# Cross-attention on one core: values two heads behind the scores, more heads multiplied whole

## The reference, cut to what matters

```python
scores = jnp.einsum('bhqd,bhkd->bhqk', q, k) * scale
probs = jax.nn.softmax(scores, axis=-1)
out = jnp.einsum('bhqk,bhkd->bhqd', probs, v)
out = out.transpose(0, 2, 1, 3).reshape(b, sq, DIM)
return out @ Wo
```

## Time and profile before

| what | value |
|---|---|
| median of 3 runs | 2446.28 us |
| profiled execution: its own time | 2448.94 us |
| profiled execution: span | 2447.2 us |
| granted TensorE clock, mean of the span | 0.995 |
| TensorE matmul busy | 2396.4 us (98%) |
| VectorE, ScalarE, GpSimd busy | 1272.9, 1049.7, 1382.5 us |
| `attend_pass` in the span | about 1840 to 2223 us |

### The profile page before, as it was taken

The page is one execution under the profiler, slowest core; times in us unless marked ns, Lnnn a source line. Parts: engine busy times, 40 slices in busy tenths (PEclk is TensorE's granted clock), DMA queues, the critical chain, the costliest instruction groups (busy, mean ns, idle before and its releaser), DMA issues. The chain is left out here.

```text
span 2447.2 us, 33141 instructions
## 1 busy us (share of the span) xinstructions
PE 2396.4 (98%) x12798; PEld 2098.0 (86%) x12798; DVE 1272.9 (52%) x1791; ACT 1049.7 (43%) x1542; POOL 1382.5 (56%) x627
## 2 busy tenths in 40 slices
PE   9999999999999999999999999999999999999998
PEld 9999999988899989999889999899986777666776
DVE  5862303862016940039720069434547899895666
ACT  2112234533337342346333363323327888882111
POOL 5434244865446855448655468444437999981221
PEclk9999999999999999999999999999999999999999
DMA  7656632334323333323333323378986776767763
GB/s 227 190 173 183 195 118 91 108 118 131 119 95 104 127 109 113 113 95 112 117 124 118 104 97 110 93 217 267 293 239 173 196 207 191 200 169 192 179 169 99
DMA packets 256158, 371.74 MB, mean 152 GB/s; under 512 B 127200, under 2 KB 179424, under 8 KB 255744
## 3 DMA queue, kind: packets, MB, share of 16 engines
q1 hardware_dynamic: 256000, 369.61, 50.4%
HBM read 290.15 MB, written 78.70 MB: 151 GB/s over the span
## 5 line engine op out<-in xcount | busy, mean ns | idle before, releaser
L1028 POOL TENSOR_TENSOR gp_w_lo<-cy_raw,gp_w_hi 128x1024 fp32r<-128x1024 f32 (+2 forms) x299 | 721.6, 2415 | 609.0 <-ACT gp_w_hi L903 608.5
L187 PE MATMUL gp_acc<-gp_x_hi,gp_w_hi 128*128 128x448 f32 x1504 | 558.0, 371 | 2.6 <-ACT gp_row L954 2.5
L189 PE MATMUL gp_acc<-gp_x_hi,gp_w_lo 128*128 128x448 f32 x1504 | 549.7, 365 | 0.0
L188 PE MATMUL gp_acc<-gp_x_lo,gp_w_hi 128*128 128x448 f32 x1504 | 549.6, 365 | 0.0
L903 ACT CAST gp_w_hi<-cy_raw 128x1024 fp32r<-128x1024 f32 (+2 forms) x300 | 307.1, 1026 | 313.1 <-PE gp_acc L189 307.5
L1511 POOL TENSOR_TENSOR ap_e_lo<-ap_e,ap_e_hi 125x1344 fp32r<-125x1344 f32 x104 | 317.2, 3092 | 9.9 <-DVE ap_e_hi L1593 6.9
L187 PEld LDWEIGHTS gp_acc<-gp_x_hi,gp_w_hi 128*128 128x128 f32 x1504 | 282.7, 188 | 25.8 <-ACT gp_row L954 4.0
L189 PEld LDWEIGHTS gp_acc<-gp_x_hi,gp_w_lo 128*128 128x128 f32 x1504 | 282.5, 188 | 22.1
L188 PEld LDWEIGHTS gp_acc<-gp_x_lo,gp_w_hi 128*128 128x128 f32 x1504 | 282.9, 188 | 20.9
L514 DVE TENSOR_REDUCE gp_sel_unit<-gp_keys 112x4 f32<-112x2048 f32 x4 | 9.1, 2286 | 548.4 <-ACT gp_keys L915 548.4
L187 PE MATMUL gp_acc<-gp_h_hi,gp_w_hi 128*128 128x448 f32 (+1 forms) x704 | 267.9, 381 | 8.4 <-DVE gp_h_lo L1091 5.6
(11 more groups left out here) (222 smaller groups left out, 4307.2 us busy)
## 6 DMA issues: line engine op xcount, KB each, us to landing
cy_raw<-in_w_gu SPq DMA_DIRECT2D x172, 512.0 KB, 3.2
cy_raw<-in_w_d SPq DMA_DIRECT2D x80, 512.0 KB, 3.5
cp_c_raw<-in_ctx_t SPq DMA_DIRECT2D x30, 750.0 KB, 6.7
cy_raw<-in_w_q SPq DMA_DIRECT2D x32, 512.0 KB, 4.5
q_scratch<-gp_q_out SPq DMA_DIRECT2D x64, 224.0 KB, 6.1
cy_qs<-q_scratch SPq DMA_DIRECT2D x64, 224.0 KB, 3.4
k_scratch<-cp_k_out SPq DMA_DIRECT2D x32, 376.0 KB
cy_ks<-k_scratch SPq DMA_DIRECT2D x64, 188.0 KB, 4.0
```

The lines of the kernel that those rows point to most:

```text
L187: nc.tensor.matmul(out, wh, xh, start=first, stop=False)
L188: nc.tensor.matmul(out, wh, xl, start=False, stop=False)
L189: return nc.tensor.matmul(out, wl, xh, start=False, stop=last)
L1028: last = nc.gpsimd.tensor_tensor(o, i, hi.bitcast(F32), ALU.subtract)
```

## The change

- `LAG` goes from 3 to 2: in the slot of head g TensorE multiplies the values of head g - 2. `take` and `put_o` follow from the same constant.
- `FULL` becomes `WHOLE`, the number of a head's blocks that are multiplied whole, the last ones of the head: 3 for head 3 as before, and 1 for head 7. In the last batch heads 1, 3, 5 and 7 are whole.
- `parts(g)` is the number of split blocks. `e_hi` and `e_lo` are made for those blocks only. `values` goes through a list: first the whole blocks, then `e_hi`, then `e_lo`. A head with one whole block has five matmuls, one in the first step and two in each of the others.
- `invert` goes from x = 22 to x = 20, behind `max_lo` and so ahead of `split_hi` of head 6; `put_recip` stays at h = 7.

```diff
-    LAG = 3
+    LAG = 2
-    RECIP_AT = 22
+    RECIP_AT, RECIP_PUT_AT = 20, 7
-    FULL, FULL_LAST = (3,), (3, 7)
+    WHOLE, WHOLE_LAST = (0, 0, 0, 3, 0, 0, 0, 1), (0, 3, 0, 3, 0, 3, 0, 3)
...
+    def parts(g):
+        return KT - (WHOLE if g // KV < B - 1 else WHOLE_LAST)[g % KV]
     def split(g):
-        return g % KV not in (FULL if g // KV < B - 1 else FULL_LAST)
+        return parts(g) > 0
...
-                nc.scalar.copy(e_hi[g % NHI][:], e[g % NE][:]).then_inc(hi_act, 1)
+                t = slice(0, parts(g))
+                nc.scalar.copy(e_hi[g % NHI][:, t], e[g % NE][:, t]).then_inc(hi_act, 1)
...
+                    if x == TURN_AT + 2 and n + 1 < B:
+                        max_lo(n + 1)
                     if x == RECIP_AT and n % GB == 0 and n > 0:
                         invert(n // GB - 1)
-                    if x == TURN_AT + 2 and n + 1 < B:
-                        max_lo(n + 1)
...
             def values(g, i):
+                s, vb, po = parts(g), vs[n % 2], p_o[g % 2][0:VW, 0:T]
+                todo = [(0, t) for t in range(s, KT)] + [(1, t) for t in range(s)] + [(2, t) for t in range(s)]
+                bounds = {KT: (0, 2, 4, 6), KT - 1: (0, 1, 3, 5), 0: (0, 1, 2, 3)}[s]
...
+                for z in range(bounds[i], bounds[i + 1]):
+                    kind, t = todo[z]
+                    if z == 0 and kind == 0:
+                        pe.wait_ge(exped, KT * (g + 1))
+                    if kind == 1 and t == 0:
+                        await_hi(pe, g)
+                    if kind == 2 and t == 0:
+                        await_lo(pe, g)
```

More of the change, by code:

```diff
@@ L1485, in _ @@
                         put_o((KV * n + h - LAG) // 2 - 1)
-                    if h == RECIP_AT // KT and n % GB == 0 and n > 0:
+                    if h == RECIP_PUT_AT and n % GB == 0 and n > 0:
                         put_recip(n // GB - 1)
@@ L1510, in _ @@
                         pool.wait_ge(pv, g - NLO + 1)
-                    nc.gpsimd.tensor_tensor(e_lo[g % NLO][:], e[g % NE][:], e_hi[g % NHI][:].bitcast(F32),
+                    t = slice(0, parts(g))
+                    nc.gpsimd.tensor_tensor(e_lo[g % NLO][:, t], e[g % NE][:, t], e_hi[g % NHI][:, t].bitcast(F32),
                                             ALU.subtract).then_inc(lo_pool, 1)
@@ L1526, in exp @@
                 if x % KT == 0 and g >= NE:
-                    if not split(g - NE):
+                    if parts(g - NE) < KT:
                         act.wait_ge(pv, g - NE + 1)
@@ L1592, in split_hi @@
                     dve.wait_ge(hi_dve, upto(hi_by_dve, g) - 1)
-                nc.vector.tensor_scalar(e_hi[g % NHI][:], e[g % NE][:], 1.0, None, ALU.mult, ALU.add,
+                t = slice(0, parts(g))
+                nc.vector.tensor_scalar(e_hi[g % NHI][:, t], e[g % NE][:, t], 1.0, None, ALU.mult, ALU.add,
                                         accum_out=e_sum[:]).then_inc(hi_dve, 1)
@@ L1610, in split_lo @@
                 dve.wait_ge(pv, g - NLO + 1)
-                nc.vector.tensor_tensor(e_lo[g % NLO][:], e[g % NE][:], e_hi[g % NHI][:].bitcast(F32),
+                t = slice(0, parts(g))
+                nc.vector.tensor_tensor(e_lo[g % NLO][:, t], e[g % NE][:, t], e_hi[g % NHI][:, t].bitcast(F32),
                                         ALU.subtract).then_inc(lo_dve, 1)
@@ L1675, in values @@
                         pe.wait_ge(o_taken, g - 1)
[L1676 to L1681, removed]
-                        await_lo(pe, g)
-                    part = e_hi[g % NHI] if z < KT else e_lo[g % NLO]
-                    last = nc.tensor.matmul(p_o[g % 2][0:VW, 0:T], vs[n % 2][:, z % KT, h, :], part[:, z % KT, :],
-                                            start=(z == 0), stop=(z == 2 * KT - 1))
+                for z in range(bounds[i], bounds[i + 1]):
[5 more added lines that the diff above has]
+                    if kind == 2 and t == 0:
+                        await_lo(pe, g)
+                    flags = {"start": z == 0, "stop": z == len(todo) - 1}
+                    if kind == 0:
+                        last = nc.tensor.matmul(po, vb[:, t, h, :].bitcast(F32), e[g % NE][:, t, :], **flags)
+                    else:
+                        part = e_hi[g % NHI] if kind == 1 else e_lo[g % NLO]
+                        last = nc.tensor.matmul(po, vb[:, t, h, :], part[:, t, :], **flags)
                 if i == KT - 1:
```

## The result

The changed kernel takes 2513.8 us in the median of four runs (2510.8 to 2516.2), against 2446.1 for the kernel before: a ratio of 1.0274, 95% interval 1.0261 to 1.0286. It is slower by 67.7 us where 52.9 were forecast. 2513.8 lies inside the stated range of 2474 to 2524, and 0.8 us above 2513, the upper bound that the prediction gave the closed path by itself. The profiled execution took 2510.8 us, with a span of 2509.0; it is the fastest of the four.

The account below looks back on a forecast made before the run. GpSimd was taken to bound the attention pass, TensorE a close second; with LAG = 2 latency would decide. 55.2 + 1.3 - 5.4 + 1.8 = +52.9 us on 2446.3 gives 2499 us, range 2474 to 2524.

Parts of the forecast that it names:

- the closed path: Attention pass: scores, exponential, e_hi, e_lo, values, scores two heads on; 27.0 us a batch, bounds 2487 and 2513.
- four links: Closed path, heads 6 to 0, 0 to 2, 2 to 4, 4 to 6: 6.33, 7.4, 6.5 and 6.5 us.
- The other signs: Steady batches: GpSimd about 81% busy, TensorE waiting some 4.5 us a batch for e_lo, no pairs waiting for maxima.
- the clock of 1.00: TensorE's granted clock: forecast to stay at 1.00 in the changed kernel.
- SP's stores move by nothing: SP's queue: put_recip stays at h = 7, put_o moves to other slots with room; no cost.
- Reciprocals: Three instructions of 0.84 us ahead of e_hi of head 6, 0.2 of it hidden: 3 x 0.6 = +1.8 us.
- +55.2: Steady batches: 14 batches going from 23.06 to 27.0 us each, +55.2 us.
- First and last batch: Start of the pass, later first turn: +1.3 us; end, one head less in the tail and VectorE freed: -5.4 us.
- Throughput decides: Rival, attention pass: e_lo comes in time, subtraction 2.1 us, TensorE's 22.4 us is the batch; 2432 us, 6%.
- The subtraction gets faster: Rival, GpSimd's subtraction: 2.6 us as engines thin out, batch of 25.2 us; 2474 us, 7%.
- The clock falls: Rival, TensorE: standing lowers the granted clock once a batch, up to 25 us more; 2523 us, 8%.

Follow-up runs that it names:

- e3_v_early: The changed kernel with the load of the values issued at h = 4 in place of h = 7: 2499.3 us, ratio 1.0209.
- e1_lag3: The changed kernel with LAG back at 3, all other parts of the change kept: 2435.9 us, ratio 0.9949.
- e2_only_lag2: The kernel before with LAG = 2 and nothing else changed: 2519.6 us, ratio 1.0291.
- e4_short_lo: e3_v_early with GpSimd subtracting only each split head's first block, which TensorE's other e_lo matmuls read again: 2437.4 us, ratio 0.9959.
- e7_lag3_last_as_before: e1_lag3 with the last batch's whole heads as before, 3 and 7 only: 2435.4 us, ratio 0.9969.
- e8_lag2_recip22: e3_v_early with the reciprocals at x = 22 again in place of x = 20: 2500.9 us, ratio 1.0234.

## Why the prediction was right

**The closed path.** Right in its parts and in its sum: four links predicted at 26.75 and 27.0 with the queue, measured 26.95, and 26.93 to 27.01 in 13 batches of e3_v_early. Only the last 0.2 is partly luck: it was put down to `e_lo` of head 5 holding up head 6, and that is some 0.05 us (e3_v_early); three of the links are 0.07 to 0.1 us longer than counted, one 0.06 shorter. e1_lag3 and e2_only_lag2 pin the loss on LAG, and e4_short_lo pins it on the length of the links. The other signs came too: in e3_v_early GpSimd is busy 80.5% (81 forecast), TensorE stands 3.9 us a batch (4.5 forecast), for six `e_lo` a batch, and no pair waits 0.1 us or more for maxima. Only the clock of 1.00 did not come in the changed kernel, where it was 0.97.

**What was missed.** "SP's stores move by nothing: ... on a queue with room" looked at what SP stores, and not at what it loads. Of a lag that shrinks, the load of the values is a part: TensorE needs them one head sooner. And the other slots of `put_o` were not without effect: its two stores now stand ahead of the load and delay its issue by 1.47 us. No run changed that order alone, so how much of the loss is theirs is open. The late load was worth 9.9 us in the profiled execution, with the clock that fell behind the longest stands. This sum is not a fixed price: e2_only_lag2 issues the load just as late, and its stands for it are 0.94 us or less.

**Reciprocals.** The step that three instructions of 0.84 us "now stand ahead of `e_hi` of head 6, which lies on the closed path", +1.8, was wrong: they cost nothing at x = 20. At x = 22 they had cost 2.3 us, which are in the mean of 23.06 and so in the +55.2 already; the term ought to have been nothing. The batch with the reciprocal had rows of its own before, 0.7 to 1.0 us longer than its neighbours, and I had taken one mean, 23.06, over all.

**First and last batch.** +1.3 was forecast for the first; measured +0.1, but the moment at which the pass starts differs more than that from one trace to the next (first turns at 1854 to 1867 us), so this term was not to be tested. The last was forecast at -5.4 and measured -5.1. I named the shorter tail first and a VectorE freed of two subtractions second; it is the other way round. With LAG = 3 and the whole heads the end is 29.1 us (e1_lag3), no longer than with LAG = 2, and without them 33.8 (e7_lag3_last_as_before). VectorE's longest subtraction there is 3.48 us, as before, and 1.56 in the changed kernel. It goes with GpSimd's first subtraction for `finish_pass`; the kernel before, then the changed one:

```profile
2211.49 2.36 POOL L1514 TENSOR_TENSOR cy_o_lo<-cy_num,cy_o_hi 128x1024 fp32r<-128x1024 f32 x1 [18.25 <-ACT cy_o_hi L1568]
2211.77 3.49 DVE L1611 TENSOR_TENSOR ap_e_lo<-ap_e,ap_e_hi 125x1344 fp32r<-125x1344 f32 x1
```

```profile
2278.53 1.56 DVE L1620 TENSOR_TENSOR ap_e_lo<-ap_e,ap_e_hi 125x1344 fp32r<-125x1344 f32 x1
2279.66 2.64 POOL L1520 TENSOR_TENSOR cy_o_lo<-cy_num,cy_o_hi 128x1024 fp32r<-128x1024 f32 x1 [18.97 <-ACT cy_o_hi L1575]
```

The one that starts second is the longer for it, VectorE's before and GpSimd's after.

**Sum.** Forecast 55.2 + 1.3 - 5.4 + 1.8 = 52.9; measured in the traces 67.7 + 0.1 - 5.1 = 62.7, the spans differing by 61.8. The 9.8 us between the two sums look like the 9.9 of the load, but only because the rest cancels: +2.8 for the first interval and +0.3 for the last batch against -1.8, -1.2 and -0.3 for the reciprocals, the first batch and the eight plain intervals. By the medians the forecast was short by 14.6 us (2499.2 against 2513.8): 8.9 by the spans, and the other 5.7 because the profiled execution before lay 2.9 us above its median and the one after 3.0 below. The time lies in the range because the range had been widened for the falling clock; for the load that made the excess nothing had been set aside, and in that the range was lucky.

**Rivals.** *Throughput decides* had the right conditional: with a short subtraction (1.15 us) LAG = 2 gives 2437 us, near its 2432; the 2.1 us that it named as the point was not run. *The subtraction gets faster* is out, at 3.07 us with GpSimd 78% busy. *The clock falls* was right as to a fact and for the most part wrong as to its cause: it fell six times, five of them behind stands of 1.7 to 3.1 us for a load and once behind 1.64 us for `e_lo`, and not once a batch by frequent short ones, of which e3_v_early has as many at a clock of 1.00. The rule quoted there from the Trainium skill (TensorE: Matmul & The Clock Gate, "A second HAM failure mode: psum-queue depth-cycling"), that frequent short idle times make the clock swing, is not borne out by these stands, of some 4 us in each batch and up to 1.3 us at a time. But one of the 14 stands of 1.26 to 1.28 us in e8_lag2_recip22 was followed by a fall, so stands of this size are not safe either.

## What to carry to other kernels

When a pipeline's lag is cut, don't compare busy times; add up the latency from a step back to itself, hand-overs included, and count the heads it spans. Where the sum exceeds the bound engine's time for as many heads, the lag is too short, whatever the busy shares say. Then list everything whose due time the lag sets, the loads too: what was issued one stage ahead may now be late. And look at what the lag moves on the queue that issues the loads, since a store that changes its slot can come to stand ahead of one.

## What the runs showed of the hardware

- TensorE stood 54 of 379 us, once for 1.64 us and else for 1.3 or less, and kept the full clock (e3_v_early: 1.00). After each of five stands of 1.7 to 3.1 us in the changed kernel the granted clock was near 0.5 for about 3 us, after each of three of 2.03 or 2.04 us in e2_only_lag2 for about 6 us; that kernel's other stands for `e_lo`, up to 1.57 us and one of 1.64, had no such fall. The stand of 1.64 us at the start of the pass was followed by a fall in one of the four traces with LAG = 2 that have it.
- GpSimd's subtraction of 125 x 1344 elements takes 3.07 to 3.09 us whether GpSimd is 98% or 78% busy; 896 elements take 2.10 and 448 take 1.15. Cutting one in two costs 0.13 us.
- Where a subtraction on VectorE and one on GpSimd overlap, the one that starts second takes longer: VectorE's 3.49 and 3.48 us in place of 1.56 when it started 0.3 us after GpSimd's (before, e7_lag3_last_as_before), GpSimd's 2.64 and 2.95 in place of 2.36 when it started 1.1 and 0.8 us after VectorE's (changed kernel, e1_lag3). VectorE's `e_hi`, with one input, took 1.54 us beside GpSimd's subtraction.
- The load of the values issued at 2092.24 let TensorE go on at 2100.74 only, 8.5 us later; the one issued at 2011.33 did so at 2017.25, after 5.9. In 13 batches it was 5.9 to 8.5 us, so in this pass the issue of a load tells little of when it lands.
